# Three of Q's eight blocks from exact codes, with Q's sum and Q's upper half taken earlier in a step

## The reference

```python
q = hidden_states @ _dequant(q_codes, q_scales)      # (code - 8) * scale per 128 rows and column
q = _rope(q); k = _rope(k)
scores = jnp.einsum('bhqd,bhkd->bhqk', q, k) * scale + mask[None, None]
attn = jax.nn.softmax(scores, axis=-1)
out = jnp.einsum('bhqk,bhkd->bhqd', attn, v)
...
x = x + _L0_attn_ref(_layernorm(x, axis=-1), ...)
x = x + _L0_xattn_ref(_layernorm(x, axis=-1), ctx_4096, ...)
x = x + _L0_ffn_ref(_layernorm(x, axis=-1), L0_ffn_weight)
```

## Time and profile before

| what | value |
|---|---|
| median of 3 runs | 1050.31 us (1050.20 to 1050.74) |
| the profiled execution itself | 1050.22 us |
| its span | 1048.4 us |
| PE busy | 1015.7 us (97%) |
| DVE busy | 902.7 us (86%) |
| POOL busy | 788.9 us (75%) |
| ACT busy | 774.4 us (74%) |

### The profile page before, as it was taken

How to read it: one execution, slowest core, us unless ns; L and a number is a source line. 1 busy time by engine, 2 the same in 40 slices (tenths; PEclk the granted TensorE clock), 3 DMA queues, 4 the chain that set the end, 5 groups by cost and what they waited for, 6 DMA issues and landing times.

```text
span 1048.4 us, 18487 instructions
## 1 busy us (share of the span) xinstructions
PE 1015.7 (97%) x5296; PEld 500.5 (48%) x5296; DVE 902.7 (86%) x1651; ACT 774.4 (74%) x1712; POOL 788.9 (75%) x833
## 2 busy tenths in 40 slices
PE   5999998999999999999999999999999999989998
PEld 3444343445555555555555455545555554454443
DVE  7989997699888888888888889999999998887773
ACT  5547766888898888888888888888888887473210
POOL 3678787899878887887888789999999999332200
PEclk9999999999999999999999999999999999999999
DMA  9783301676887676667667766777787765534442
GB/s 337 258 199 121 116 26 34 145 152 157 161 162 166 138 165 158 147 152 159 165 138 165 157 147 140 153 165 150 156 150 156 160 138 113 118 122 96 88 96 74
DMA packets 309804, 152.01 MB, mean 145 GB/s; under 512 B 257728, under 2 KB 274240, under 8 KB 309728
## 3 DMA queue, kind: packets, MB, share of 16 engines
q1 hardware_dynamic: 301952, 137.76, 58.0%
q10 hardware_dynamic: 7776, 13.37, 4.5%
HBM read 85.26 MB, written 4.19 MB: 85 GB/s over the span
## 4 chain that ended last, share of the span: by engine, by line
PE 82%; DVE 6%; POOL 5%; ACT 3%; issue 2%; DMA 1%; ACTq 0%; SPq 0%; DVEq 0%; POOLq 0%
PE out_ps L969 10%; PE proj_ps L969 9%; PE side_ps L949 9%; PE side_ps L757 8%; PE side_ps L759 8%; PE side_ps L758 8%; PE side_ps L845 5%; PE proj_ps L1130 5%; PE score_ps L932 3%; PE score_ps L933 3%; PE score_ps L934 3%; PE proj_ps L1135 2%; PE score_ps L1100 2%; PE out_ps L780 1%; PE proj_ps L757 1%
## 5 line engine op out<-in xcount | busy, mean ns | idle before, releaser
L1687 POOL TENSOR_SCALAR prob<-prob,row_inv 128x512 f32<-128x512 f32 (+3 forms) x256 | 196.7, 779 | 81.9 <-DVE row_inv L2224 80.3
L1694 POOL TENSOR_TENSOR w_b<-prob,w_b 128x896 f16<-128x896 f32 (+2 forms) x192 | 186.0, 995 | 6.5 <-ACT w_b L1373 6.4
L1346 ACT ACTIVATE prob<-score_ps,neg_max 128x512 f32<-128x512 f32 (+3 forms) x256 | 132.9, 526 | 30.7 <-DVE neg_max L2141 29.1
L2154 DVE SCALAR_TENSOR_TENSOR x_acc<-out_ps,o_now,x_acc 128x1024 f32<-128x1024 f32 x120 | 153.1, 1276 | 1.3 <-PE out_ps L969 1.3
L2154 DVE SCALAR_TENSOR_TENSOR x_acc<-proj_ps,o_now,x_acc 128x1024 f32<-128x1024 f32 x120 | 153.0, 1275 | 0.0
L757 PE MATMUL side_ps<-hT,w_a 128*128 128x512 f16 x384 | 145.5, 379 | 0.5 <-ACT side_ps L1313 0.2
L759 PE MATMUL side_ps<-hT,w_a 128*128 128x512 f16 x384 | 145.5, 379 | 0.0
L758 PE MATMUL side_ps<-hT,w_a 128*128 128x512 f16 x384 | 145.5, 379 | 0.0
L2141 DVE CUSTOM_DVE_ANT_0 score_ps<-score_ps,mask_b 128x512 f32<-128x512 f32 (+3 forms) x256 | 122.7, 501 | 16.9 <-PE score_ps L934 16.6
L969 PE MATMUL proj_ps<-work,w_b 128*128 128x512 f16 x496 | 127.3, 379 | 1.9 <-DVE x_acc L2154 1.5
L969 PE MATMUL out_ps<-work,w_b 128*128 128x512 f16 x496 | 127.3, 379 | 0.8 <-DVE x_acc L2154 0.7
(11 more groups left out here) (276 smaller groups left out, 2230.1 us busy)
## 6 DMA issues: line engine op xcount, KB each, us to landing
stage_c<-in_codes_dram SPq DMA_DIRECT2D x72, 256.0 KB, 2.9
stage_o<-in_codes_dram SPq DMA_DIRECT2D x64, 256.0 KB, 3.3
stage_s<-in_scales_dram SPq DMA_DIRECT2D x34, 256.0 KB, 3.7
ctx_raw<-in_ctx_dram ACTq DMA_DIRECT2D x32, 256.0 KB, 3.2
work<-w_b SPq DMA_TRANSPOSE x261, 3.1
x_acc<-in_x_dram SPq DMA_DIRECT2D x8, 512.0 KB, 8.9
k_sb<-in_codes_dram SPq DMA_DIRECT2D x16, 256.0 KB, 7.0
v_sb<-in_scales_dram SPq DMA_DIRECT2D x16, 256.0 KB, 7.4
```

The costliest lines, as they stand in the source:

```text
L1346: ins = act.activation(prob[:, SCORE_AT[qb]:SCORE_AT[qb] + w], score_ps[:, score_bank(i, u), off:off + w], ACT.Exp, bias=neg_max[:, c:c + ...
L1687: return pool.tensor_scalar(prob[:, at:at + w], prob[:, at:at + w], row_inv[:, col:col + 1], P_UP, ALU.mult, ALU.mult)
L1694: ins = pool.tensor_tensor(prob16[:, 1, to:to + w], prob[:, at:at + w], prob16[:, 0, to:to + w], ALU.subtract)
L2154: ins = dve.scalar_tensor_tensor(y, u, s, y, ALU.mult, ALU.add)
```

## The change

Seven edits go together.

1. `N_EXACT` is 3, so three blocks of Q are computed from exact codes: 3 x 2 + 5 x 3 = 21 matmuls for a Q head and batch entry in place of 22, with three steps of `q_base` on ScalarE. The piece in even slots is 128 columns wide in place of 256, and its table of ratios is made in ten steps in place of seven.
2. On TensorE the three `q_exact` lie further apart, and the second score unit is split around one of them; o1 moves ahead of the third score unit.
3. On VectorE `q_sum` stands ahead of the third maxima and so ahead of the first reciprocal.
4. On ScalarE `q_hi` stands ahead of the third exponentials, and the second `q_base` ahead of the first exponentials.
5. In slots 8 to 39 VectorE shifts the context's codes (after the second reciprocal) in place of ScalarE, and o0's addition stands behind the first reciprocal. In all other slots it stays ahead of it.
6. The last tile of K is finished at other places of slots 0 to 2.
7. The small ratio table lies in another tile's space.

Two multiplications stand ahead of the first exponentials, Q's upper half ahead of the third, and the shift of the codes is gone. The core of the diff:

```diff
-N_EXACT = 2
+N_EXACT = 3
+RATIO_STEPS = 3 * N_EXACT + 1
@@ TensorE, slot
-                scores(p, i, g, 1)
+                scores(p, i, g, 1, slice(0, 1))
                 if has_ahead and parts:
                     q_exact(*ahead, 1)
+                scores(p, i, g, 1, slice(1, 2))
...
+                if has_ahead and parts:
+                    q_exact(*ahead, 2)
...
+                if has_o and not (known(p) and p == O_LAG):
+                    o_unit(p, i, 1)
                 scores(p, i, g, 2)
@@ ScalarE, slot
                 if has_ahead and by_parts(p + Q_AHEAD):
                     q_base(*next_q, 0)
+                if has_ahead and by_parts(p + Q_AHEAD):
+                    q_base(*next_q, 1)
                 exps(p, i, 0)
...
                 exps(p, i, 1)
+                if has_next and by_parts(p + 1):
+                    q_hi(p + 1)
...
                 exps(p, i, 2)
-                if with_ctx:
-                    act.wait_ge(ctx_scaled, q + 1)
-                    act.activation(dst, ctx_codes, ACT.Copy, bias=-Q_MID).then_inc(ctx_free, 1)
@@ VectorE, slot
                 maxima(p, i, 1)
+                if not with_ctx:
+                    first_add()
+                if has_next and by_parts(p + 1):
+                    q_sum(p + 1)
                 maxima(p, i, 2)
-                if has_o:
-                    ...
-                    o_add(p, i, 0)
                 dve.wait_ge(exp_done, p * 3 + 2)
                 dve.reciprocal(row_inv[:, 0:3], row_sum[:, 0:3]).then_inc(inv_ready[0], 1)
-                if has_next and by_parts(p + 1):
-                    q_sum(p + 1)
+                if with_ctx:
+                    first_add()
...
+                if with_ctx:
+                    q, dst = ctx_half(g, i)
+                    dve.wait_ge(ctx_scaled, q + 1)
+                    dve.tensor_scalar(dst, ctx_codes, Q_MID, None, ALU.subtract).then_inc(ctx_free, 1)
```

More of the change, by code:

```diff
@@ L107 @@
 RATIO_FROM = 4
-RATIO_STEPS = 7
 CB = D // P
@@ L912, in v_blocks, with scores @@
                     v_group(V_HERE + n // KB, n % KB)
-            def scores(p, i, g, u):
+            def scores(p, i, g, u, part=slice(None)):
                 b, r = i % B, score_bank(i, u)
@@ L921, in scores @@
                         pe.wait_ge(k_rest, K_TILES * K_BY_DVE)
-                    if known(p) and p == O_LAG:
+                    if known(p) and p == SLOTS - 1:
                         pe.wait_ge(k_ready, K_TILES)
                     pe.wait_ge(q_ready, p + 1)
-                if not (known(p) and 3 * p + u < 2):
+                units = SCORE_UNITS[u][part]
+                if units[0] == SCORE_UNITS[u][0] and not (known(p) and 3 * p + u < 2):
                     pe.wait_ge(exp_done, p * 3 + (u - 1))
-                for qb, off in SCORE_UNITS[u]:
+                for qb, off in units:
                     w = (qb + 1) * P
@@ L1027, in slot @@
                 if has_o:
-                    if not first_o:
-                        o_unit(p, i, 1)
                     o_unit(p, i, 2)
@@ L1450, in slot @@
                 exps(p, i, 2)
+                if known(p) and p == 1:
+                    late_swaps()
+                if known(p) and p == 2:
+                    late_upper()
                 if with_ctx:
@@ L2076, in ratio_step @@
                     dve.wait_ge(scale_rows_landed, 32)
+                e = (k - 3) // 3
                 if k == 0:
[L2078 removed]
+                    ins = dve.tensor_tensor(by, of, of, ALU.mult)
                 elif k == 1:
@@ L2081, in ratio_step @@
                 elif k == 2:
-                    ins = dve.tensor_tensor(by, by, rows[:, :, 1], ALU.add)
-                elif k == 3:
-                    ins = dve.reciprocal(per, by)
-                elif k == 4:
-                    ins = dve.tensor_tensor(per, rows[:, :, 0], per, ALU.mult)
-                else:
-                    row, up = ((per, 1.0), (by, Q_UP))[k - 5]
-                    c = CB + k - 5
+                    ins = dve.tensor_tensor(by, by, of, ALU.add)
+                elif k < RATIO_STEPS - 1 and k % 3 == 0:
+                    ins = dve.reciprocal(per, by[:, :, e])
+                elif k < RATIO_STEPS - 1 and k % 3 == 1:
+                    ins = dve.tensor_tensor(per, by[:, :, e - 1] if e else rows[:, :, 0], per, ALU.mult)
+                else:
+                    row, up = (per, 1.0) if k < RATIO_STEPS - 1 else (by[:, :, N_EXACT - 2], Q_UP)
+                    c = CB + e
                     dve.tensor_scalar(o_table[:, 0:NH - Q_LEAD, c], row[:, Q_LEAD:NH], up, None, ALU.mult)
@@ L2172, in ao_rest, with slot @@
                     .then_inc(ao_ready, 1)
-            def slot(g, i):
+            def slot(g, i, with_ctx):
                 p = g * SLOTS + i
@@ L2238, in slot @@
                     wf_difference(wf_early(p))
+                if known(p) and 0 < p < 3:
+                    (late_sum, late_lower)[p - 1]()
                 if has_o:
@@ L2248, in body @@
                 for i in range(SLOTS):
-                    slot(g, i)
+                    slot(g, i, with_ctx)
             def x1_part():
```

49 lines of the change are left out of this document (22 added, 27 removed).

## The result

The changed kernel takes 1053.51 us (median of 8 runs, 1053.0 to 1053.69) against 1050.45 (8 runs, 1050.15 to 1050.84): a ratio of 1.0028, 95% interval 1.0019 to 1.0038. It is slower, by 0.28%. The forecast said 1048.0 and gave most weight to faster; the time lies inside the range, on the other side of before.

The account below looks back on a forecast made before the run. TensorE was taken to bound the kernel, without gaps, each slot costing its matmuls' 11.46 us. Terms -13.0 + 7.2 + 1.6 + 1.4 + 0.6 = -2.2 took 1050.2 to 1048.0 us; range 1040 to 1057.

Parts of the forecast that it names:

- The matmul that goes: TensorE: 21 matmuls in place of 22 for 60 Q tiles in slots 2 to 61, 13.0 us less.
- Weight slots: Slots 40 to 59: VectorE's second reciprocal waits through q_sum and q_hi; slots of 11.6, not 11.24, 7.2 us given back.
- The leg through GpSimd: Weight slots: loop of normalisation, GpSimd's work to the sine, q_sum, third maxima, reciprocal; 11.75 less 0.3, so 11.45 us.
- Loop slots: Slots 8 to 39: o1 waits 0.1 us for o3's late addition in every second slot, 1.6 us given back.
- The round trip fits, by 0.1: Loop slots: second multiplication ends at 3.78, third exact block starts at 3.89 us into the slot; priced at nothing.
- The shift's price: Loop slots: shifting the context's codes on VectorE takes about 0.6 us.
- Rival 3: Loop: VectorE's shift stands behind GpSimd's q_lo, 0.6 us a pair of slots, 1056.0 us; chance 0.08.
- Early slots: Slots 3 to 6 run the weight slots' new loop: five slots' gain, 1.1, and 0.3 us given back.
- The end: Tail after the last slots: TensorE waits for VectorE's additions and keeps the reciprocal's lateness, 0.6 us given back.
- rival 2: Weight slots: new loop loses more than is gained elsewhere, sign turning from 11.71 us a slot; 1055.4 us; chance 0.20.
- Rival 4: Exact blocks: the round trip's 0.1 is lost, TensorE waits about 0.2 us in 33 slots, 1055 us; chance 0.05.
- Rival 1: All slots: TensorE keeps the pace, weight slots at 11.24 us; 1038.6 us; chance 0.17.

Follow-up runs that it names:

- run 1: Changed kernel, but outside the loop Q's sum stands behind the first reciprocal and Q's upper half behind the third exponentials: 1047.78 us.
- run 2: Changed kernel, but outside the loop only Q's upper half stands behind the third exponentials on ScalarE again; VectorE keeps the sum early: 1048.65 us.
- run 5: Changed kernel, but in the loop's odd slots VectorE scales the weight piece ahead of o0's addition: 1049.25 us.
- run 4: Changed kernel with all its orders, but two exact blocks and two multiplications, so 22 matmuls for a Q tile: 1067.98 us.
- run 7: Changed kernel, but the moved conversions of slots 1 and 2 stand at their old places on ScalarE and VectorE: 1053.58 us.
- run 9: Changed kernel, but in slots 61 and 62 alone Q's sum stands behind the first reciprocal and Q's upper half behind the third exponentials: 1052.34 us.
- run 12: Kernel of run 11, but in slot 40 alone the FFN weight's difference stands ahead of o1's addition again: 1039.86 us.
- run 11: Changed kernel with edits of run 1 and run 5, o1 behind third scores in slots 62 and 63, and o1's addition before FFN difference outside loop: 1040.34 us.

## Why the prediction was wrong

The step that failed first is the price of the loop slots: 1.6 forecast and 3.9 measured. Its path was wrong: ScalarE waits for the piece's scaling, and TensorE for ScalarE at the second exact block. Then come the end, 0.6 and 2.3, and the early slots, whose net is +1.4 and not +0.1. Of the gain of 13.0, 10.8 was to be given back (7.2, 1.6, 1.4, 0.6) and 16 was; that turned the sign. The largest item was right in mechanism and nearly in size. The misses are 2.3 in the loop, 1.3 in the early slots, 0.8 in slots 60 and 61, 1.7 at the end and 0.2 in the weight slots, less 1.1 ahead of slot 0. Their sum of 5.2 is larger than the gain that was left (2.2).

- *The matmul that goes*, -13.0: right. Slots without a wait last 11.25.
- *Weight slots*, 7.2 given back: right. Slots 40 to 59 give +3.1 against a forecast of +2.9, with the idle time before the second reciprocal that the step named (0.64, forecast 0.7), and runs 1 and 2 take the loss away by undoing what the step blamed. The leg through GpSimd, which was not the one taken, was overrated: the normalisations shrank by 0.69 and 0.42, and not by 0.3, and GpSimd waited 1.48 and not at most 1.25. The rate should have been charged in slots 60 and 61 too. They have no weight piece, but they have the sum, `q_hi` and the difference: +0.8 over the forecast.
- *Loop slots*, 1.6 given back: the term that failed most, 3.9 in its place (32 x 0.216 = 6.9 less the 3.0 gained). The step counted the right slots, every second one, and 0.1 in each, at o1, where 0.25 were lost. 0.08 of it is at o1. The other 0.17 is at the second exact block, where the step saw nothing. It followed VectorE's lateness to o3's addition directly. What carries it is ScalarE, by way of the piece's scaling: I had the first reciprocal 0.5 later (it is 0.6) and asked only who waits behind the last addition, not who waits for the operation between. "The round trip fits, by 0.1" was asked of the third block, and that one does come in time; the second doesn't, because the first multiplication comes late. Run 5 gives all of the 3.9 back, and 0.3 in slots 40 to 59.
- *The shift's price.* I took about 0.6; it took 1.24 to 1.30. Rival 3's mechanism is thus real, but not its price: in run 5 the shift is 1.25 to 1.35 and the loop loses nothing.
- *Early slots*, +0.1 net: +1.4. Slot 0, which makes no block from exact codes, lasts 11.24 instead of 10.87; run 4, with two blocks and a shorter ratio table, has 10.87 again. Slots 5 to 7 lose 0.9 by the early sum and upper half (35.07 against 34.14 in run 1). Slots 2 to 4 take 0.3 more than before and not less. That is not explained; run 7 shows only that the moved conversions don't cause it.
- *The end*, 0.6: 2.3. I took it for VectorE's additions, which the row before names, and they are what it follows: 159.3 us from o1's addition in slot 62 to the end in every profile that keeps their order. The size was wrong. The step charged the lateness of the reciprocal. But o3's addition is 1.1 late already, and the loop of the weight slots closes once more: VectorE idles 1.03 before the second reciprocal, behind the sum and `q_hi`. Run 9 gives 0.7 of the stretch back; 1.6 stays with the sum and `q_hi` late.
- *Up to slot 0*, nothing forecast: -1.1. TensorE waits less for an addition in the K tiles, 2.1 us and not 3.8. That comes with the ratio table's new steps, which stand among VectorE's work there (run 4: -0.2); which of them shifts what was not tried.

No rival's account is the measured one. Weight slots of 11.65 stay under rival 2's 11.71. Rival 4's waits at an exact block are there, 0.17 in the even slots 10 to 40 and 0.52 in the odd weight slots. But the round trips alone don't cause them: run 5 keeps all three and has loop slots of 11.25, and run 1 odd weight slots of 11.25. Rival 1 has 1038.6; run 12, with the places found here mended and run 11's edit besides, which the changed kernel has not, comes to 1039.9.

## What to carry to other kernels

An engine at 89% can be the one that sets the pace: what counts is whether its operations between two hand-overs have slack (run 5 has ScalarE at 90% and loses nothing). So for each operation made later, ask who waits for it first, not only for the last in the row. When a change shortens the bounding engine by 2%, price every place where another engine is within 2%, the ends and the short stretches too; here five of six stretches came out above the forecast. And when a bundle of reorderings comes with a gain, undo them one by one: here one was needed outside the loop (o0's addition), one cost 4.9 us there (`q_hi`), and one lacked its partner (the scaling).
